# Mixing stage: sending the routed rows one group step later from two buffers, with the step loops written out

## The reference

```python
y = _layer_norm(x + _mha(x, Wqkv, bqkv, Wo, bo), g1, be1)     # x: the layer-normed input of this part
z = _layer_norm(y + _moe(y, Wg, W1, b1, W2, b2), g2, be2)
...
def _mha(x, ...):      # S, B, _ = x.shape : here the 8 sequences attend to each other, per position, 4 heads of 64
def _moe(x, ...):
    logits = xf @ Wg.T
    idx = jnp.argmax(logits, axis=-1)                          # one of 8 experts per row
    for e in range(E):
        m = (idx == e)[:, None].astype(xf.dtype)
        h = jax.nn.relu(xf @ W1[e] + b1[e])
        out = out + m * (h @ W2[e] + b2[e])
```

## Time and profile before

| | us |
|---|---|
| median of 3 runs | 1274.46 (1273.99 to 1275.9) |
| the profiled execution, its own time | 1278.25 |
| its span, first to last instruction | 1276.2 |
| attention, 0 to 699 | 699.00 |
| mixing, 717.05 (first scores) to 976.35 | 259.30 |
| experts, 976.35 to the end | 299.85 |

### The profile page before, as it was taken

One profiled execution on the slowest core, in us unless ns is written; L12 is line 12 of the kernel. 1 busy time (PEld: TensorE's weight loads), 2 busy tenths in 40 slices (PEclk: granted clock), 3 DMA queues, 4 the chain that ended last, 5 costly groups with the idle time before them and its releaser, 6 DMA issues. The chain is left out here.

```text
span 1276.2 us, 27822 instructions
## 1 busy us (share of the span) xinstructions
PE 1169.9 (92%) x8837; PEld 795.8 (62%) x8845; DVE 758.6 (59%) x2126; ACT 530.1 (42%) x1123; POOL 472.4 (37%) x679
## 2 busy tenths in 40 slices
PE   8999899999999999999888799999877999999996
PEld 3546455464654646546444466666655999999996
DVE  3555567756678576774354366566662556656564
ACT  5445354544545445454432354444421323333230
POOL 3334325244253442533420123344331344444444
PEclk8999899999999999999899899999987999999999
DMA  7214524143240432403121164434344111111110
GB/s 212 70 43 117 141 71 121 28 113 104 70 128 20 113 104 73 123 12 101 49 58 52 33 215 161 136 132 148 123 142 175 53 52 54 48 53 55 52 50 8
DMA packets 114210, 115.27 MB, mean 90 GB/s; under 512 B 29868, under 2 KB 100271, under 8 KB 114032
## 3 DMA queue, kind: packets, MB, share of 16 engines
q1 hardware_dynamic: 108816, 100.53, 27.4%
q0 software_dynamic: 4512, 12.92, 2.6%
q10 hardware_dynamic: 832, 1.19, 0.3%
HBM read 53.60 MB, written 23.30 MB: 60 GB/s over the span
## 5 line engine op out<-in xcount | busy, mean ns | idle before, releaser
L958 ACT ACTIVATE probs<-ps_b 128x512 f32<-128x512 f32 (+2 forms) x352 | 174.5, 537 | 94.3 <-PE ps_b L1275 38.0
L581 POOL TENSOR_SCALAR_AFFINE_SELECT probs<-probs 128x512 f32<-128x512 f32 x128 | 81.7, 638 | 269.8 <-ACT probs L958 265.8
L2756 PE MATMUL ps_c<-keep_w,e_hT 128*128 x624 | 141.0, 379 | 0.0
L2756 PEld LDWEIGHTS ps_c<-keep_w,e_hT 128*128 128x128 f32 x624 | 115.7, 190 | 14.1
L700 DVE CUSTOM_DVE_ANT_0 ps_a<-ps_a,mask_qk 128x256 f32<-128x256 f32 x224 | 89.0, 452 | 20.3 <-PE ps_a L1244 20.2
L2712 ACT ACTIVATE e_w_now<-keep_w 128x1024 f32 x78 | 78.3, 1051 | 33.3 <-PEq L1945 21.0
L694 DVE TENSOR_REDUCE top<-ps_a 128x2 f32<-128x512 f32 (+1 forms) x112 | 74.2, 684 | 28.1 <-PE ps_a L1244 27.3
L1244 PE MATMUL ps_a<-k_rows,q_rows 96*128 96x256 bf16 (+1 forms) x512 | 84.5, 260 | 4.6 <-DVE top L700 2.7
L2716 ACT ACTIVATE e_yT<-ps_d 128x256 f32<-128x256 f32 x39 | 15.0, 384 | 169.1 <-PE ps_d L2735 169.1
L1275 PE MATMUL ps_b<-q_rows,k_rows 98*128 98x256 bf16 (+1 forms) x512 | 76.7, 264 | 0.2
L2745 PE MATMUL ps_a<-e_yT,e_w_now 128*128 128x128 f32 x640 | 74.7, 275 | 0.0
(11 more groups left out here) (248 smaller groups left out, 2417.4 us busy)
## 6 DMA issues: line engine op xcount, KB each, us to landing
q_rows<-parts SPq DMA_DIRECT2D x96, 128.0 KB, 2.4
k_rows<-parts SPq DMA_DIRECT2D x96, 128.0 KB, 2.4
q_rows<-q_parts SPq DMA_DIRECT2D x96, 128.0 KB, 2.4
e_row<-sorted_rows SPq DMA_DIRECT2D x39, 258.0 KB, 2.6
keep_w<-in_e_w SPq DMA_DIRECT2D x16, 512.0 KB, 4.2
keep_w<-in_e_w SPq DMA_DIRECT2D x8, 1024.0 KB, 7.9
x_in<-in_x SPq DMA_DIRECT2D x8, 512.0 KB, 3.9
x_res<-in_x SPq DMA_DIRECT2D x8, 512.0 KB, 4.6
```

Source lines behind the costliest of these rows:

```text
L581: nc.gpsimd.affine_select(own, own, [[0, TILES], [1, P]], ALU.is_ge, keep_zero, base=0, channel_multiplier=-1).then_inc(probs_cut.sem, 1)
L958: nc.scalar.activation(probs[:, user % 2, lo:lo + width], ps_exp[:, f % 2, 0:width], ACT.Exp).then_inc(exp_done.sem, 1)
L2756: mm = nc.tensor.matmul(ps_out[:, s, 0:D], hT[:, s, f, :], w2[:, bass.ds(e * KF * D + f * D, D)], start=(f == 0), stop=(f == KF - 1))
```

## The change

- `rows`, `slot`, `rows_loaded` and `rows_sent` exist twice; group n-1 uses side (n-1) % 2.
- POOL's four sends of group n-2 come in step n, after a wait for the second half of `yT` of step n, instead of the sends of group n-1 after `slots(n)` at the end of step n. The sends of the last two groups follow after step 7 and after step 8's own work.
- The waits for landed sends (VectorE's `post_norm_apply`, POOL's row numbers, SP's `load_rows`) look at the sends of the same side, two groups back.
- `mixed` is now a view of `kT`'s buffer, and `yT` a view of `mixed` (its half h lies on tiles 2h and 2h+1).
- VectorE does `normalise(n, 0)` ahead of `mix(n, 0)` and `normalise(n, 1)` ahead of `mix(n, 1)`.
- The loops of SP, POOL, VectorE and TensorE over the steps are written out; ScalarE's loop stays.
- SP sends all ten spare filler tiles; POOL sent the first of them before.

```diff
-        mixed = sb("m_mixed", [P, TILES, D])
-        rows = sb("m_rows", [P, TILES, ROW])
-        yT = sb("m_yT", [P, KD, S])
+        mixed = kT[:, :, :].rearrange("p k (c d) -> p (k c) d", c=2)
+        rows = sb("m_rows", [P, 2, TILES, ROW])
...
+        def yT_half(h):
+            return mixed[:, KD * h:KD * (h + 1), :]
...
                     load_expert(n)
-                    if not (isinstance(n, int) and n == 0):
-                        sp.wait_ge(rows_sent.sem, rows_sent.count(n, 16 * TILES))
+                    if n >= 2:
+                        sent = rows_sent[n % 2]
+                        sp.wait_ge(sent.sem, sent.count(n // 2, 0))
                     load_rows(n)
...
-                with sp.Fori(1, NGROUPS - 2) as n:
-                    iteration(n, True)
-                iteration(NGROUPS - 2, False)
-                iteration(NGROUPS - 1, False)
+                for n in range(1, NGROUPS):
+                    iteration(n, n < NGROUPS - 2)
...
+                def number_rows(n):
+                    if n >= 3:
+                        sent = rows_sent[(n - 1) % 2]
+                        wait_apart(pool, pool_passed, sent.sem, sent.count((n - 1) // 2, 0))
+                    wait_apart(pool, pool_passed, token_next.sem, token_next.count(n, 0))
+                    nc.gpsimd.tensor_copy(rows[:, (n - 1) % 2, :, 2 * D], token[:, :]).then_inc(token_written.sem, 1)
...
+                def send_rows(n):
+                    loaded = rows_loaded[(n - 1) % 2]
+                    wait_apart(pool, pool_passed, loaded.sem, loaded.count((n - 1) // 2, 16 * B))
+                    wait_apart(pool, pool_passed, y_ready.sem, y_ready.count(n, TILES))
+                    wait_apart(pool, pool_passed, slot_ready.sem, slot_ready.count(n, 1))
+                    for c in range(TILES):
+                        nc.gpsimd.indirect_dma_start(
+                            out=t["sorted"], out_offset=bass.IndirectOffsetOnAxis(ap=slot[:, (n - 1) % 2, c:c + 1], axis=0),
+                            in_=rows[:, (n - 1) % 2, c, :], in_offset=None).then_inc(rows_sent[(n - 1) % 2].sem, 16)
...
-                with pool.Fori(1, NGROUPS - 2) as n:
-                    iteration(n)
-                for n in (NGROUPS - 2, NGROUPS - 1):
-                    iteration(n, more=False)
+                iteration(0)
+                iteration(1)
+                for n in range(2, NGROUPS):
+                    iteration(n, more=n < NGROUPS - 2)
+                    pool.wait_ge(yT_ready.sem, yT_ready.count(n, 2))
+                    send_rows(n - 1)
+                send_rows(NGROUPS - 1)
                 iteration(NGROUPS, work=False, more=False)
+                send_rows(NGROUPS)
...
                 def post_norm_apply(n, k, own):
-                    dve.wait_ge(rows_sent.sem, rows_sent.count(n, 0))
+                    if n >= 3:
+                        sent = rows_sent[(n - 1) % 2]
+                        dve.wait_ge(sent.sem, sent.count((n - 1) // 2, 0))
...
                     maxima(n, 1)
+                    normalise(n, 0)
                     if route:
                         mix(n, 0)
-                    normalise(n, 0)
+                    normalise(n, 1)
                     if route:
                         mix(n, 1)
-                    normalise(n, 1)
...
-                with dve.Fori(1, NGROUPS - 2) as n:
+                for n in range(1, NGROUPS - 2):
                     iteration(n)
...
-                with pe.Fori(1, NGROUPS - 1) as n:
+                for n in range(1, NGROUPS - 1):
                     iteration(n)
```

More of the change, by code:

```diff
@@ L1818, in mixing_program @@
         slot_f = sb("m_slot_f", [P, TILES])
-        slot = sb("m_slot", [P, TILES], U32)
+        slot = sb("m_slot", [P, 2, TILES], U32)
         next_row = sb("m_next_row", [P, 2, E])
@@ L1841, in mixing_program @@
         x_loaded = signal("m_x_loaded", 16 * B, -16 * B)
-        rows_loaded = signal("m_rows_loaded", 16 * B)
+        rows_loaded = [signal(f"m_rows_loaded{side}", 16 * B) for side in range(2)]
         ln_stats = signal("m_ln_stats", TILES)
@@ L1883, in mixing_program @@
         token_next = route_signal("m_token_next", 1, 1)
-        rows_sent = route_signal("m_rows_sent", 16 * TILES, 16)
+        rows_sent = [signal(f"m_rows_sent{side}", 16 * TILES) for side in range(2)]
         filler_sent = signal("m_filler_sent", 0)
@@ L1956, in load_rows @@
                     for s in range(B):
-                        sp.dma_start(rows[s * POS:(s + 1) * POS, :, D:2 * D],
-                                     t["x2_groups"][m, s].rearrange("(c i) d -> i c d", i=POS)).then_inc(rows_loaded.sem, 16)
+                        sp.dma_start(rows[s * POS:(s + 1) * POS, m % 2, :, D:2 * D],
+                                     t["x2_groups"][m, s].rearrange("(c i) d -> i c d", i=POS)).then_inc(rows_loaded[m % 2].sem, 16)
                 def load_expert(e):
@@ L2000, in _ @@
                 nc.gpsimd.memset(ones16[:, :], 1.0).then_inc(consts_set.sem, 1)
-                nc.gpsimd.memset(rows[:, :, 2 * D:ROW], 0.0).then_inc(consts_set.sem, 1)
+                nc.gpsimd.memset(rows[:, :, :, 2 * D:ROW], 0.0).then_inc(consts_set.sem, 1)
                 nc.gpsimd.memset(filler[:, :], 0.0).then_inc(consts_set.sem, 1)
@@ L2020, in post_norm_rstd @@
                     nc.gpsimd.tensor_tensor(rstd1[:, own], veps1[:, own], half[:, own], ALU.pow).then_inc(ln1_rstd.sem, 1)
-                def iteration(n, work=True, route=True, more=True):
+                def number_rows(n):
[4 more added lines that the diff above has]
+                    nc.gpsimd.tensor_copy(rows[:, (n - 1) % 2, :, 2 * D], token[:, :]).then_inc(token_written.sem, 1)
+                    wait_apart(pool, pool_passed, token_written.sem, token_written.count(n, 1))
+                    nc.gpsimd.tensor_scalar(token[:, :], token[:, :], float(TILES * POS), None,
+                                            ALU.add).then_inc(token_next.sem, 1)
@@ L2023, in iteration @@
+                def iteration(n, work=True, more=True):
                     if work:
                         for h in range(2):
-                            if route:
+                            if n > 0:
                                 pool.wait_ge(mixed_ready.sem, mixed_ready.count(n, h + 1))
                             bias(n, h)
-                    if route:
+                    if n > 0:
                         for k, own in enumerate(post_norm_parts(n)):
                             post_norm_rstd(n, k, own)
[L2031 to L2037, removed]
+                        number_rows(n)
@@ L2038, in iteration @@
                     if more:
                         ln_first(n + 2)
[L2040 to L2047, removed]
@@ L2058, in _ @@
+                for n in range(2, NGROUPS):
[3 more added lines that the diff above has]
+                send_rows(NGROUPS - 1)
                 iteration(NGROUPS, work=False, more=False)
-                pool.wait_ge(rows_sent.sem, rows_sent.count(NGROUPS, 16 * TILES))
+                send_rows(NGROUPS)
+                for sent in rows_sent:
+                    pool.wait_ge(sent.sem, sent.count(NGROUPS // 2, 0))
@@ L2122, in post_norm_apply @@
                     dve.wait_ge(ln1_scaled.sem, ln1_scaled.count(n, own.stop))
-                    dve.wait_ge(rows_sent.sem, rows_sent.count(n, 0))
+                    if n >= 3:
+                        sent = rows_sent[(n - 1) % 2]
+                        dve.wait_ge(sent.sem, sent.count((n - 1) // 2, 0))
                     for c in range(own.start, own.stop):
-                        nc.vector.scalar_tensor_tensor(rows[:, c, 0:D], mixed[:, c, :], rstd1[:, c:c + 1], be1[:, :],
+                        nc.vector.scalar_tensor_tensor(rows[:, (n - 1) % 2, c, 0:D], mixed[:, c, :], rstd1[:, c:c + 1], be1[:, :],
                                                        ALU.mult, ALU.add).then_inc(y_ready.sem, 1)
@@ L2159, in slots @@
                     dve.wait_ge(slot_f_ready.sem, slot_f_ready.count(n, 1))
-                    nc.vector.tensor_copy(slot[:, :], slot_f[:, :]).then_inc(slot_ready.sem, 1)
+                    nc.vector.tensor_copy(slot[:, (n - 1) % 2, :], slot_f[:, :]).then_inc(slot_ready.sem, 1)
                     dve.wait_ge(next_row_ready.sem, next_row_ready.count(n, 1))
@@ L2429, in y_features @@
                                 col = P * (2 * k + i)
-                                mm = nc.tensor.transpose(ps[:, col:col + P], rows[:, 2 * h + i, k * P:(k + 1) * P], identf[:, :])
+                                mm = nc.tensor.transpose(ps[:, col:col + P], rows[:, (n - 1) % 2, 2 * h + i, k * P:(k + 1) * P], identf[:, :])
                         mm.then_inc(work_full.sem, 1)
```

13 lines of the change are left out of this document (5 added, 8 removed).

## The result

The changed kernel takes **1267.11 us** (median of 4 runs, 1266.48 to 1268.42), the kernel before, run beside it, 1275.18 (1273.99 to 1276.0). The ratio is 0.9943, 95% interval 0.9928 to 0.9958: faster, by 8.1 us. The forecast was 1264.5 with a range of 1258.5 to 1270.0. The profiled execution after took 1267.25, its span is 1265.6; before it was 1278.25 and 1276.2. So the profiles differ by 10.6 us of span and the medians by 8.1: the profiled run of before lay 3 us above its median, that of after on it.

The account below looks back on a forecast made before the run. TensorE was taken to bound each step, with late signals beside the sends and POOL-VectorE collisions adding waits. Terms -6.0, -3.8, -3.2, -1.0 make -14.0; +4.0 gives -10.0, so 1274.5 becomes 1264.5 us, range 1258.5 to 1270.0.

Parts of the forecast that it names:

- The sends leave the scores: Routing steps: second maxima follow as in step 1, and the first transposes' 1.39 us wait for normalise goes.
- A full step of 27.4: Each full step: 27.38 + 0.15 - 0.13 = 27.4 us; steps 2 to 5 go from 115.6 to 109.6, -6.0.
- The one stretched product in four: VectorE, each step: POOL's first bias meets normalise(n, 1), which takes 1.77 us for 0.69, 1.08 once.
- the 0.13 for the loop: TensorE's back edge: writing out the loop saves 0.13 us of loop arithmetic in a full step.
- The second collision at nothing: POOL's second bias beside the statistics of mixed: costs nothing; bound 1.08 us per step, 6.5 in all.
- The other bound, VectorE first: VectorE's product ahead of POOL's bias in a step: gives back 0.4 us per step.
- Steps 6 and 7: Step 6 falls from 31.16 to 27.4 us, -3.8; step 7 loses 3.2 of 3.6 us of TensorE's idling, -3.2.
- The parts at nothing: Shared keys' buffer, SP's extra filler, SP's loads of rows and POOL's wait for yT: no cost.
- The sends' new place, +4.0: Sends behind yT, beside the keys: k1's signal held, losing 0.8 us five times; bounds nothing and 10.
- Rival 1: No late signals at the sends' new place: 1274.5 - 14.0 = 1260.5 us; chance 0.29.
- The closing, -1.0: post_norm_apply(8) waits for POOL's rstd instead of landed sends, group 6's sends making it some 0.5 us later: saves 1.0.
- rival 2: Late signals are partly the profiler's, so the runs have less to lose: 1268.3 us; chance 0.17.

Follow-up runs that it names:

- a_old_place: The changed kernel with the sends back at the end of their own step; 1271.25 us.
- g_bias_second: d_close with POOL's first bias also held until normalise(n, 1) has its scale, so VectorE's product is first; 1259.75 us.
- d_close: The changed kernel with the first four of the eight closing sends moved behind POOL's part of the last step; 1261.04 us.
- b_old_order: The changed kernel with VectorE's mix ahead of normalise again; 1288.63 us.
- e_plain: The changed kernel with eight added plain writes of 258 KB on SP's queue at the sends' old place, steps 2 to 7; 1263.5 us.
- k_pool_plain: The changed kernel with four added plain writes of 258 KB on POOL's queue at the sends' old place, steps 2 to 7; 1274.93 us, one run.
- h_one_old: The changed kernel with one of a group's four sends (tile 0) back at the old place; 1263.82 us.
- i_two_old: The changed kernel with two of a group's four sends (tiles 0 and 1) back at the old place; 1269.24 us.

## Why the prediction was right, and where it was not

The direction and the range hold; by terms, against the profiles:

- **The sends leave the scores**: right. Maxima, transposes and the 1.39 us wait went as told. a_old_place brings the late maxima and the longer steps back, with the wait at the values rather than at the transposes.
- **A full step of 27.4**: measured 27.50. Steps 2 to 5 gave 5.6 for the 6.0 foretold. The one stretched product in four and the features as the next late thing (0.79 us) are there, and so is the 0.13 for the loop: the scores start 0.10 us after the end of the keys' copy, for 0.23 before (882.62 and 888.22).
- **The second collision at nothing**: right; the statistics beside the bias keep 1.41 us for four. The other bound, VectorE first, was put at 0.4 a step and is 0.86 (27.50 to 26.64 in g_bias_second).
- **Steps 6 and 7**: the sizes came out, 3.7 for 3.8 and 3.0 for 3.2, but not by the waits alone. The rows had clocks of 0.95 and 0.93; the text names the first and puts no price on either. 1.76 us of step 6's gain and 1.40 of step 7's are TensorE's busy time; of the 3.2 us of idling that step 7 was to lose, 1.6 went (3.61 to 2.02). That the changed kernel has no such stretch in step 6, and less of one in step 7, was luck.
- **The parts at nothing**: right. In step 5 POOL's first send (877.03) waits for nothing but its own issue, and SP's waits for landed sends fell from 133.8 us in 7 waits to 85.7 in 6, while VectorE's waits for `x_in`, loaded behind them, stay at 1.9 us in all (1.7 before).
- **The sends' new place, +4.0**: this step failed. The bound was worked out from two late signals by their distance in time from the first send, as if the sends held every signal of TensorE. They do not: `k0` and `k1` come as before, and `m_oT` at 879.92 follows its product at once although a send began at 879.75. Rival 1 was right in the steps. By the Trainium skill, "SBUF — State Buffer", section "Who interferes with whom", a DMA never contends with a compute engine; the new place agrees with that. At the old place TensorE computes on time too, but its signal comes late beside sends by indices, by 0.55 to 2.1 us, and what the prediction drew from the rule, that sends cost nothing, does not hold there; the measurement decides.
- **The closing, -1.0**: this step failed too, at +2.2. It named the one thing that hurts ("POOL now sends group 6 just ahead of group 7"), but as a later rstd on POOL, and gave it 0.5 us. Eight sends one after the other take 10 us, and beside them TensorE's signal for the second `mix` came 3.3 us late; the rstd held nothing up. The saving behind the `mix` is there, 2.2 us for the 1.0 foretold. The projection at the lower clock, +1.27, was in no term. d_close takes away 5.45 us by moving one line.

The two misses are +4.0 that did not come and 3.2 that did, and nearly cancel: foretold -10.0, the profiles -10.6. The forecast lies 2.6 us below the median, as the profiled run of before was 3 us above its own median; rival 2 (part of the late signals is the profiler's) would look the same, and no run tells it from chance, since medians of before moved between 1274.5 and 1277.1 from one set of runs to the next.

Shares of the change: the order alone gives 7 us; the written-out loops alone cost 12 (they let POOL go first, and brought stretches of low clock); the moved sends give 1.5 us in a step, and lose at the closing. With the new order the loops cost little: a_old_place, with both and the sends at their old place, has a ratio of 0.9962 to before, the order alone 0.9945, and their intervals overlap.

**Left open**: what in the sends by indices delays the signal, and why it meets the second scores and, behind eight sends, the last projection, but neither `k0`, `k1`, the logits nor the last values at the new place with the same four sends around them. The late projection signal is there in every run that issues eight in a row across the product's end (3.2 to 3.3 us in after, b_old_order and e_plain, 1.9 in k_pool_plain); why h_one_old, with seven and the last of them under way at that end, has its second `mix` only 0.41 us behind the product was not followed up. What brings on the stretches at the lower clock was not separated either: TensorE was busy without a gap in the 1.9 us before that of b_old_order's step 3, and the full-clock steps after it have the same waits.

## What to carry to other kernels

Before moving a transfer, look at what it will run beside at both ends of the loop, the last pass above all, where two passes' transfers come together: that was worth more than all that was feared in the middle. Try each part of a change alone; here four lines of order gave as much as the whole, and one part cost 1%. Where two engines hold each other up, 0.03 us decided who came first, so fix the order with a wait instead of leaving it to the shape of the loops.

## What the runs showed of the hardware

- Sends by indices, issued by POOL so that at least the second of them lies near the end of TensorE's second scores, delayed the signal of these scores by 0.55 to 2.1 us, in pieces of some 0.6 to 0.7, in every step with such sends but step 2 of a_old_place and i_two_old; eight plain writes at 243 GB/s beside the same scores delayed nothing.
- A product of two SBUF tiles on VectorE (128x512) takes 0.69 us alone or when it is first by 0.06 us or more, and 1.77 to 1.79 when POOL's bias began 0.03 to 0.04 us earlier. The one exception: in step 2 of a_old_place a product that began 0.14 us ahead of the bias took 1.98; POOL's last send was still being issued then. The Trainium skill, "SBUF — State Buffer", section "Who interferes with whom", says that whoever issues first blocks the other fully; the rows agree. That an instruction of VectorE with at most one SBUF input, outside its two-port modes, does not contend, as the same section says, fits the statistics (1.41 us beside the bias).
- One stretch of 3.4 us at the lower clock level costs a step 1.6 to 1.7 us (30.82 and 29.12 in b_old_order, 28.27 and 26.64 in g_bias_second).
